# Group 1 of layer 0's attention on layer 1's PSUM banks and SBUF tiles, in a fused two-layer stack

## What is computed

```python
x = x + tanh(g_xattn[0]) * L0_xattn(layernorm(x), ctx, ctx, ...)   # 16 heads of 8, q and k l2-normalised, scores squared
x = x + tanh(g_ffn[0])   * L0_ffn(layernorm(x), w_gate, w_up, w_down)   # blockwise fp4 of x, h and weights; silu(gate)*up
x = x + tanh(g_xattn[1]) * L1_xattn(layernorm(x), ctx, ctx, mask, ...)  # one head, masked softmax
x = x + tanh(g_ffn[1])   * L1_ffn(layernorm(x), ...)   # self-attention of 16 heads, then top-2 of 8 experts, two layer norms
```

## Time and profile before

| | us |
|---|---|
| median of 3 runs | 771.22 (770.91 to 774.88) |
| the profiled execution | 774.85 |
| its span in the trace | 772.4 |
| TensorE busy | 674.0 (87%) |
| VectorE busy | 537.1 (70%) |
| ScalarE busy | 412.7 (53%) |

### The profile page before, as it was taken

How to read it: one execution, slowest core, us unless ns; L and a number is a source line. 1 busy time by engine, 2 the same in 40 slices (tenths; PEclk the granted TensorE clock), 3 DMA queues, 4 the chain that set the end, 5 groups by cost and what they waited for, 6 DMA issues and landing times.

```text
span 772.4 us, 18073 instructions
## 1 busy us (share of the span) xinstructions
PE 674.0 (87%) x7536; PEld 463.6 (60%) x7536; DVE 537.1 (70%) x1150; ACT 412.7 (53%) x680; POOL 215.3 (28%) x543
## 2 busy tenths in 40 slices
PE   3395685887699999999999999999999999998983
...
PEclk9656567999689999999999999999999999999997
...
DMA packets 23967, 12.59 MB, mean 16 GB/s; under 512 B 6408, under 2 KB 23376, under 8 KB 23888
## 3 DMA queue, kind: packets, MB, share of 16 engines
...
## 4 chain that ended last, share of the span: by engine, by line
PE 77%; DVE 9%; ACT 6%; POOL 3%; issue 2%; DMA 2%; POOLq 0%; SPq 0%; DVEq 0%
PE A L876 20%; PE B L876 17%; PE Y L876 15%; PE H L876 15%; PE B L1119 4%; PE A L880 3%; PE B L880 2%; DMA cin<-in_ctx_dram 2%; ACT A L394 1%; ACT hid L394 1%; ACT xn L399 1%; PE A L1015 1%; POOL hs L319 1%; DVE stats L604 1%; ACT hT L405 1%
## 5 line engine op out<-in xcount | busy, mean ns | idle before, releaser
L876 PE MATMUL H<-xmT,w_s 128*128 128x512 f32 x256 | 137.4, 618 | 7.8 <-ACT hid L394 7.8
L394 ACT ACTIVATE hid<-H,b_s 128x512 f32<-128x512 f32 x128 | 87.7, 685 | 95.0 <-PE H L876 94.5
L309 POOL TENSOR_TENSOR hs<-stats 128x4 f32<-128x4 f32 x48 | 16.9, 353 | 427.7 <-DVE stats L604 427.6
L876 PEld LDWEIGHTS Y<-w_s,hid 128*128 128x128 f32 x1024 | 121.3, 192 | 19.9 <-issue 17.2
L876 PE MATMUL Y<-w_s,hid 128*128 128x128 f32 x1024 | 126.4, 277 | 2.2 <-DVE acc L853 1.4
L853 DVE SCALAR_TENSOR_TENSOR acc<-Y,wgt,acc 128x128 f32<-128x128 f32 x256 | 71.8, 343 | 48.9 <-PE Y L876 48.4
L876 PE MATMUL A<-wguT,xTq 128*128 128x352 f32 x128 | 53.5, 547 | 7.2 <-DVE hh L704 4.8
L876 PEld LDWEIGHTS H<-xmT,w_s 128*128 128x128 f32 x256 | 39.0, 189 | 31.6 <-ACT hid L394 18.6
L876 PE MATMUL A<-hT,kT 32*64 32x256 f32 x512 | 49.6, 462 | 9.1 <-ACT A L394 3.1
L794 DVE TENSOR_REDUCE mx<-B 128x16 f32<-128x1024 f32 x32 | 39.1, 1223 | 19.6 <-PE B L876 19.4
L319 POOL TENSOR_TENSOR hs<-hs,mhalf 128x4 f32<-128x4 f32 x48 | 50.6, 1054 | 3.8
...
## 6 DMA issues: line engine op xcount, KB each, us to landing
...
```

The costliest lines, as they stand in the source:

```text
L309: pl.tensor_tensor(w[:, 0], st[:, :, 1], st[:, :, 4], ALU.subtract)
L394: return act.activation(dst, source, f, **kw)
L876: return pe.matmul(o, l, r, start=start, stop=stop)
```

## The change

Group 1's layer-0 attention gets its own set of banks and tiles. For group 1 alone, every stage whose name begins with `a` uses B2 and B1 in place of A2 and A1, and layer 1's tiles in place of layer 0's: `xmT` for `qk`, `P4` for `A0`, `qT4`, `hT4` and `oT4` for `kT0`, `hT0` and `oX`, `pT1` for the four small tiles of `a_l2`, and a part of a new tile `pool` for `vz0`. `pool` holds what `hid` and `acc` held, and POOL clears it (128x3072) ahead of its first factors. `a_k` waits for the `a_av` of the last group with the same set instead of that of the group before.

```diff
@@ -139,7 +142,9 @@
-        hid = sb("hid", [2, FCH, N]); acc = sb("acc", [2, T, P])
+        pool = sb("pool", [2 * FCH * N + 2 * N])
+        hid = pool[:, 0:2 * FCH * N].rearrange("p (a c n) -> p a c n", a=2, c=FCH)
+        acc = pool[:, 2 * FCH * N:2 * FCH * N + 2 * N].rearrange("p (a t d) -> p a t d", a=2, t=T)
@@ -147,6 +152,27 @@
+        OTHER = (1,)
+
+        def before(g):
+
+            same = [q for q in range(g) if (q in OTHER) == (g in OTHER)]
+            return same[-1] if same else -1
+
+        set0 = dict(A2=A2, A1=A1, qk=qk, A0=A0, kT0=kT0, hT0=hT0, vz0=vz0, oX=oX, ss=ss, ssh=ssh, rs=rs, rs2=rs2)
+        set1 = dict(A2=B2, A1=B1, qk=xmT[:].rearrange("p a (t d) -> p a t d", t=T), A0=P4, kT0=qT4, hT0=hT4,
+                    vz0=pool[:].rearrange("p (x n d) -> p x n d", n=Q4, d=48),
+                    oX=oT4[:].rearrange("p (t w s) -> p t w s", t=T, w=2),
+                    ss=pT1[:, 0:NSS], ssh=pT1[:, NSS:2 * NSS], rs=pT1[:, 2 * NSS:3 * NSS], rs2=pT1[:, 3 * NSS:4 * NSS])
+
+        def of(g, name):
+            return (set1 if g in OTHER else set0)[name]
+
+        def bank_of(stage, g):
+            b = BANK[stage]
+            return {"A2": "B2", "A1": "B1"}[b] if stage[0] == "a" and g in OTHER else b
@@ -301,6 +328,7 @@
                 pl.memset(pbd[:], 0.0).then_inc(setup, 1)
+                pl.memset(pool[:], 0.0).then_inc(setup, 1)
@@ -628,58 +656,62 @@
-                    filled(ve, "a_av", g - 1)
+                    filled(ve, "a_av", before(g))
@@ -1215,159 +1247,158 @@
     "ScalarE": """
-        a_ctx:0 a_w:0 a_n1:0 a_ctx:1 a_wo:0 a_n1t:0 f_wm:0 a_sq:0 f_wd:0 f_w:0 a_kt:0 a_qt:0 a_n1:1 a_s0.0:0 a_n1t:1
+        a_ctx:0 a_w:0 a_wo:0 a_n1:0 f_wm:0 a_n1t:0 a_sq:0 f_wd:0 a_ctx:1 a_kt:0 a_qt:0 a_s0.0:0 a_n1:1 a_s0.1:0
...
```

391 lines of the change are left out of this document (198 added, 193 removed).

## The result

The changed kernel takes **760.74 us** (median of 5 runs, 756.53 to 763.88) against 771.22 of the kernel before on the same chip; the ratio of the two is 0.985, 95% interval 0.981 to 0.988. The forecast was 768.6 us with a range of 763.0 to 774.0. The profiled execution took 760.09 us (span 757.8).

A forecast was written before the change was run, and what follows sets the result against it. TensorE was nearly always busy from 240 to 640 us, so gains had to come from its gaps and slow clock in the first 240 us; terms from -4.0 to +2.1 summed to -2.6 us: 768.6 us, range 763.0 to 774.0.

The forecast's parts named there:

- The rest of the lists: All other list entries, moved by one to four places, add or remove no work: 0, with 1.5 us either side.
- Gate and up in A2: From `f_gu.0:0` to group 1's first scores, transposes in B banks fit inside the waits and `a_ctx:2` leaves: -4.0 us.
- `a_k:1` out of VectorE's way: `a_k:1` moves from before `f_gu.0:0` to VectorE's free time during group 0's scores: -1.1 us at `f_gu.0:0`.
- Group 1's scores: In group 1's layer-0 attention two `a_av` leave the gaps and stand in series on TensorE: +2.1 us.
- group 0's: In group 0's scores the gap of tile 1 holds only one of `a_av.0` and `a_n1t:1`: +1.0 us.
- the first rival: TensorE's clock rises to full within group 1's scores, each tile taking 1.40 us instead of 2.34: 764.6 us, chance 0.22.
- `a_q:1` ahead of `a_o0:0`: Before group 0's output projection, `a_q:1` is partly hidden, +1.3 us; an earlier clock rise speeds `a_o0:0`, -1.5.
- `a_o0:1` in B2: Between `f_qht:0` and `xh`, the bank waits of `a_o0:1` (0.77) and `f_dn:0` (1.01) go: -1.7 us.
- Start: At the kernel's start, reordered ScalarE entries and `a_kv:1` ahead of `a_kt:0` make `a_kt:0` later: +0.9 us.
- restart: After `f_dn:0`, `c_kv:0` and `a_ctx:2` ahead of `a_kv:2` are mostly covered by idle time: +0.4 us net.
- Given back before 240 us: From 125 to 240 us VectorE may become the bound, so the gain is lost: 771.2 us, chance 0.20.
- Slower: Group 2's restart falls at half clock, with `c_kv:0`, `a_ctx:2`, `a_kv:2`, `a_q:2` in one row: 775.2 us, chance 0.08.

The follow-up runs named there:

- early_lists_of_before: The kernel before, with its banks and its lists up to about 135 us, and the changed kernel's lists behind that: 767.7 us, ratio 0.992.
- VectorE's piece of 180 to 198 us: The kernel before with only that piece of VectorE's list from the changed kernel (`s_o.0:0`, `s_o.1:0` earlier, `f_dn:1` later, `f_qx` and `a_l2` steps swapped): 769.4 us, ratio 0.995.
- banks_only: The changed kernel's banks and tiles with the lists of the kernel before, except `c_kv:0` and `a_ctx:2` moved behind `f_dn:0`: 766.1 us, ratio 0.992.

## Why the prediction was wrong, step by step

**The rest of the lists, taken as 0 with 1.5 either way.** This is the step that failed. "Entries moved by one to four places, adds or removes no work" was true and said nothing of the time: they are worth 5.8 us at the median (`early_lists_of_before`). With -5.8 in place of 0 the sum is -8.4 and the time 762.8, already outside the range. The earlier trace rows had a clock of 0.85 and 21 us without TensorE work between 125 and 240 us. I used that row to say where a gain can lie and then did not ask which moves fall in it. VectorE's piece of 180 to 198 us makes 4.0 us of the difference by the ratio: with it GpSimd's step for `c_n3:1` takes 0.25 us instead of 2.58, and the clock stays full behind 200 us. No row of the kernel before would have named the 2.58 us of GpSimd as the thing to look for, but its row stood in the timeline that I had not opened, since I stopped at 150 us.

**Gate and up in A2, -4.0.** Right: 20.1 us became 15.75, -4.4. In other traces it takes 17.2 to 20.1 us with the banks of before and 13.3 to 15.75 with those of the change, since the clock rises sooner or later within it. What the Trainium skill, "TensorE: Matmul & The Clock Gate", section "HAM oscillation — how this bites in real kernels", reports of its kernel, that PSUM double-buffering gave no further gain, does not carry over: here the banks alone give 6.6 us.

**`a_k:1` out of VectorE's way, -1.1.** Measured -2.1 from the end of `a_o0:0` to `f_gu.0:0` (17.05 to 15.00). I halved the 2.0 us for what might be late next; in this trace nothing was.

**Group 1's scores, +2.1, and group 0's, +1.0.** Measured +0.4 for group 1's (15.21 to 15.64) and +0.7 for group 0's (15.27 to 15.98, from the first scores to the end of the last `a_av`). TensorE ran in part at the full clock from 88 to 94 us (two tiles' scores at 1.88 us for 2.34, one `a_av` at 0.65 for 1.08), which gives back 1.35 us. That is the first rival, in a third of its size; its own working gave 3.8 and its sum used 4.0. Without it the term would be +1.8, near the +2.1. In `banks_only` the first two tiles took 1.41 and 1.40 us, so there the rival came in half of its size.

**`a_q:1` ahead of `a_o0:0`, +1.3 less 1.5.** From the last `a_av` to the end of `a_o0:0` the sum had -0.2; measured -0.9 (4.45 to 3.57). The clock rose some 4 us sooner and gave `a_o0:0` 1.7 us (3.68 to 1.97), so the mechanism was right. Undone, the total is not longer.

**`a_o0:1` in B2, -1.7.** Both waits went; measured -1.0 (8.52 to 7.50), because `f_qht:0` ran at half clock (1.97 us instead of 1.38).

**Start, +0.9, restart, +0.4.** +0.4 and -0.4 (`xh` to `f_gu.0:1`, 16.89 to 16.45). Small, and both errors to the same side.

**The rivals.** "Given back before 240 us" happened in the small: 1.9 us were lost between `f_gu.0:1` and `f_dn:1`. "Slower" didn't: the clock at the restart, from 112 to 120 us, was full. It fell behind that, to a mean of 0.54 from 120 to 125, so the last sign of being wrong showed at its edge without its consequence. Of the signs of being right, the scores without idle time before them and `a_k:1` near 35 us (34.64) showed; `xh` came at 111.8 us and not near 116, and the stretch from 125 to 240 us did not keep its busy time.

Up to `f_gu.0:1` the sum had -2.6 and the trace -7.3: every term but `a_o0:1` erred to the same side, by 0.3 to 1.7 us each. That they did is not explained, and some of it can be the execution's. The halves separated on the chip say -6 for the early lists and banks and -6 for the late ones. The range was too narrow because it gave 1.5 us to 90 us of a timeline in which TensorE waits and its clock falls.
